# Attention scores and value products of a fused decoder layer in three passes of high and low operands

## What is computed

```python
qkv = jnp.einsum('bsh,ph->bsp', x, weight_qkv).reshape(b, s, NKV, GROUP)   # NKV = 4 groups
q = qkv[..., :QPG * D].reshape(b, s, NKV, QPG, D)                          # 4 query heads each, D = 128
k = qkv[..., QPG * D:(QPG + 1) * D]
v = qkv[..., (QPG + 1) * D:]
scores = jnp.einsum('bsgqd,btgd->bgqst', q, k) * scale
scores = jnp.where(causal, scores, jnp.finfo(scores.dtype).min)
attn = jax.nn.softmax(scores, axis=-1)
out = jnp.einsum('bgqst,btgd->bsgqd', attn, v)
return jnp.einsum('bse,he->bsh', out.reshape(b, s, NH * D), weight_proj)
```

## Time and profile before

| | us |
|---|---|
| median of 3 runs | 1920.68 |
| lowest and highest | 1916.56, 1920.68 |
| profiled execution, its own time | 1925.99 |
| its span, first to last instruction | 1924.0 |
| PE busy | 1846.8 (96%) |
| DVE busy | 1064.5 (55%) |
| ACT busy | 966.6 (50%) |

### The profile page before, as it was taken

The page is one execution under the profiler, slowest core; times in us unless marked ns, Lnnn a source line. Parts: engine busy times, 40 slices in busy tenths (PEclk is TensorE's granted clock), DMA queues, the critical chain, the costliest instruction groups (busy, mean ns, idle before and its releaser), DMA issues. The chain is left out here.

```text
span 1924.0 us, 28232 instructions
## 1 busy us (share of the span) xinstructions
PE 1846.8 (96%) x9769; PEld 1307.8 (68%) x9769; DVE 1064.5 (55%) x2125; ACT 966.6 (50%) x1789; POOL 283.2 (15%) x783
## 2 busy tenths in 40 slices
PE   6999999998999999998998989989989999999998
PEld 4677777776777777764544434434469999999998
DVE  7433443443433434454676867767853336776766
ACT  3533434443434444343576766767753126666651
POOL 1000000000000000042144343343210600000015
PEclk9999999999999999998999999999989999999999
DMA  3100000000100000000000033000010437887756
GB/s 142 34 1 1 23 1 34 1 1 24 34 1 1 22 1 1 1 12 1 1 1 6 2 126 140 0 0 1 1 47 1 183 112 255 291 287 276 273 171 226
DMA packets 73383, 131.54 MB, mean 68 GB/s; under 512 B 4512, under 2 KB 35232, under 8 KB 73248
## 3 DMA queue, kind: packets, MB, share of 16 engines
q1 hardware_dynamic: 68128, 113.01, 17.0%
q0 software_dynamic: 5120, 16.78, 2.6%
HBM read 96.75 MB, written 33.03 MB: 67 GB/s over the span
## 5 line engine op out<-in xcount | busy, mean ns | idle before, releaser
L1561 DVE TENSOR_REDUCE xmax<-ps 128x1 f32<-128x512 f32 x512 | 330.9, 682 | 120.2 <-PE ps L1121 111.0
L1387 ACT ACTIVATE xp<-ps 128x1024 f32<-128x1024 f32 x256 | 263.4, 1031 | 105.9 <-PE ps L1132 104.2
L1319 ACT ACTIVATE probs<-ps,nmax 128x128 f32<-128x128 f32 (+3 forms) x256 | 135.3, 528 | 298.6 <-DVE nmax L1534 297.7
L1534 DVE TENSOR_REDUCE nmax<-ps 128x1 f32<-128x128 f32 (+3 forms) x256 | 124.9, 488 | 238.5 <-PE ps L963 237.4
L1121 PE MATMUL ps<-k,q 64*128 64x512 f32 x496 | 217.5, 479 | 5.3 <-DVE xmax L1561 4.8
L1121 PEld LDWEIGHTS ps<-k,q 64*128 64x128 f32 x496 | 86.8, 188 | 170.6 <-DVE xmax L1561 134.8
L963 PE MATMUL ps<-k_t,q_t 128*128 128x128 f32 (+3 forms) x512 | 198.3, 470 | 0.0
L1132 PE MATMUL ps<-q3m,k 64*128 64x512 f32 x512 | 183.4, 455 | 0.0
L1041 PE MATMUL ps<-pt,v_s 128*128 128x128 f32 (+3 forms) x512 | 159.8, 457 | 2.2 <-ACT pt L1357 1.9
L158 PE MATMUL ps<-ident,probs 128*128 128x128 f32 x704 | 125.1, 282 | 27.3 <-DVE probs L1499 14.8
L158 PEld LDWEIGHTS ps<-ident,probs 128*128 128x128 f32 x704 | 89.6, 144 | 79.8 <-issue 46.8
(11 more groups left out here) (179 smaller groups left out, 3343.5 us busy)
## 6 DMA issues: line engine op xcount, KB each, us to landing
w_raw<-in_w_t SPq DMA_DIRECT2D x56, 704.0 KB, 6.0
w_raw<-in_w_t SPq DMA_DIRECT2D x28, 768.0 KB, 5.9
rows_x<-w_raw SPq DMA_DIRECT2D x1, 9984.0 KB, 29.9
mixed<-rows_x SPq DMA_DIRECT2D x39, 256.0 KB, 4.5
rows_y<-y_s SPq DMA_DIRECT2D x39, 256.0 KB, 5.4
w_raw<-in_w_qkv_t SPq DMA_DIRECT2D x4, 1536.0 KB, 6.8
res<-in_x SPq DMA_DIRECT2D x4, 1024.0 KB, 12.4
w_raw<-in_w_proj_t SPq DMA_DIRECT2D x4, 1024.0 KB, 5.5
```

Of the source, the lines that this page charges most:

```text
L1319: act.activation(probs[:, u % 4, 0:w], ps[:, S_BANK + u % 2, 0:w], ACT.Exp, bias=nmax[:, u % 4:u % 4 + 1], accum_out=rsum[:, u % 4:u % 4 + ...
L1387: act.activation(xp[:, kv % 2, 2 * pair:2 * pair + 2, t, :], ps[:, XST + 2 * (t % 2):XST + 2 * (t % 2) + 2, :], ACT.Exp, scale=X_SCALE).th ...
L1534: dve.tensor_reduce(nmax[:, u % 4:u % 4 + 1], ps[:, S_BANK + u % 2, 0:w], AX_X, ALU.max, negate=True).then_inc(s_max, 1)
L1561: dve.tensor_reduce(xmax[:, slot, i, h:h + 1], ps[:, bank + u % 2, :], AX_X, ALU.max, negate=True).then_inc(s_xmax, 1)
```

## The change

Every operand of the scores and of the products with the values is now kept as two float32r tensors, a high half that ACT rounds from PSUM and a low half that DVE subtracts (PSUM less the high half): `kh`/`kl`, `qh`/`ql`, `vh`/`vl`, `pth`/`ptl`. Each float32 product becomes three float32r products: high·high, high·low, low·high. PE waits for the low half (`s_ql` for a projection, `s_tl` for a turned tile or turned values), where it waited for ACT's copy (`s_q`, `s_te`). The queries have one buffer in place of two, and the turned shares lie tile after tile. The raw weights lie where `wl` and `wol` are written ("in place"), each with a place of its own; six DMAs, one a projection, take the place of one, and SP waits with each until the old low half was last used.

```diff
+            def low_chain(piece, b, bank, value):
+                dve.wait_ge(s_q, value)
+                src = ps[:, G_BANK + bank, :]
+                if piece == 0:
+                    ins = dve.tensor_tensor(kl[:, b % 2, :], src, kh[:, b % 2, :].bitcast(F32), ALU.subtract)
+                else:
+                    h = PROJ_ORDER[piece]
+                    ins = dve.scalar_tensor_tensor(ql[:, h, :], src, ATT_SCALE, qh[:, h, :].bitcast(F32), ALU.mult,
+                                                   ALU.subtract)
+                ins.then_inc(s_ql, 1)
+
+            def low_values(b, bank, value):
+                dve.wait_ge(s_te, value)
+                dve.tensor_tensor(vl[:, b % 2, :, :], ps[:, T_BANK + bank, :].rearrange("p (j d) -> p j d", j=TOK_TILES),
+                                  vh[:, b % 2, :, :].bitcast(F32), ALU.subtract).then_inc(s_tl, 1)
...
             for n in range(NPROJ):
                 split_in(n, n + 1)
+            low_chain(0, 0, 0, 1)
             moments_of(1)
...
-                pe.matmul(ps[:, S_BANK + u % 2, 0:w], q_t[:, b % 2, h, i * P:w], k_t[:, b % 2, 0:w],
-                          start=False, stop=True, skip_group_check=True).then_inc(s_s, 1)
+                for q, kk in ((qh, kh), (qh, kl), (ql, kh)):
+                    ins = pe.matmul(ps[:, S_BANK + u % 2, 0:w], q[:, h, i * P:w], kk[:, b % 2, 0:w],
+                                    start=False, stop=True, skip_group_check=True)
+                ins.then_inc(s_s, 1)
...
                     elif op[0] == "turn":
                         pe.wait_ge(s_pn, N_UNIT * g + op[1] + 1)
-                        pe.wait_ge(s_te, turns_done(g, t) - 1)
+                        pe.wait_ge(s_tl, turns_done(g, t) - 1)
...
-                        pe.wait_ge(s_te, turns_done(g, t))
+                        pe.wait_ge(s_tl, turns_done(g, t))
 
                         for j in reversed(range(TOK_TILES)):
-                            ins = pe.matmul(ps[:, O_BANK + h % 2, j * P:], v_s[:, b % 2, j, :], pt[:, j, j * P:],
-                                            start=(j == TOK_TILES - 1), stop=True, skip_group_check=True)
+                            for v, p in ((vh, pth), (vl, pth), (vh, ptl)):
+                                ins = pe.matmul(ps[:, O_BANK + h % 2, j * P:], v[:, b % 2, j, :],
+                                                p[:, 4 * j:3 * j + TOK_TILES, :].rearrange("p i n -> p (i n)"),
...
             def split_in(n, value):
+                act.wait_ge(s_wp[n], value)
                 act.copy(wh[:, :, columns(n)], w_raw[:, :, columns(n)]).then_inc(s_wh, 1)
...
+                    if op[0] == "turn":
+                        i = op[1] % TOK_TILES
+                        dve.wait_ge(s_te, turns_done(g, t) + 1)
+                        dve.tensor_tensor(ptl[:, i:4 * i + 1:3, :],
+                                          ps[:, T_BANK + (1 + t) % 2, 0:(i + 1) * P].rearrange("p (j n) -> p j n", n=P),
+                                          pth[:, i:4 * i + 1:3, :].bitcast(F32), ALU.subtract).then_inc(s_tl, 1)
+                    elif op[0] == "chain" and is_chain(op):
+                        if op[1] != "v":
+                            low_chain(piece_of(op[1]), op[2], c % 2, N_QKV * g + NPROJ + k + 1)
+                    elif op[0] == "chain":
+                        low_values(op[2], (1 + t) % 2, turns_done(g, t) + 1)
...
+            for g in range(GROUPS - 1):
+                for n in range(NPROJ):
+                    sp.wait_ge(s_g, chains_done(g, last_use(n)))
+                    sp.dma_start(w_raw[:, :, columns(n)], w_v[g + 1][:, :, columns(n)]).then_inc(s_wp[n], 16)
+
+                sp.wait_ge(s_g, chains_done(g + 1, TOK_TILES - 1))
+                sp.dma_start(wo_raw[:, :, :], wo_v[g + 1]).then_inc(s_wo, 16)
```

More of the change, by code:

```diff
@@ L131, in turns_done, with lows_of, last_use @@
     return N_TURN * g + t + 1
+def lows_of(g, k):
+    return (NPROJ - 1) * (1 + BATCH * g + k // NPROJ) + k % NPROJ - (k % NPROJ > 1)
+def last_use(piece):
+    return [c for op, c, t, k in walk(MIDDLE) if op[0] == "chain" and op[2] == BATCH - 1 and is_chain(op)][piece]
 def piece_of(name):
@@ L427, in build @@
         s_out = sem("s_out")
-        s_w = sem("s_w")
+        s_wp = [sem(f"s_wp{n}") for n in range(NPROJ)]
+        s_wo = sem("s_wo")
         s_wh = sem("s_wh")
@@ L442, in build @@
         s_q = sem("s_q")
+        s_ql = sem("s_ql")
+        s_tl = sem("s_tl")
         s_res = sem("s_res")
@@ L636, in _ @@
                 if b == 0:
[L637 to L644, removed]
+                    for n in range(NPROJ):
+                        sp.dma_start(w_raw[:, :, columns(n)], w_v[0][:, :, columns(n)]).then_inc(s_wp[n], 16)
+            sp.dma_start(wo_raw[:, :, :], wo_v[0]).then_inc(s_wo, 16)
+            for g in range(GROUPS - 1):
+                for n in range(NPROJ):
+                    sp.wait_ge(s_g, chains_done(g, last_use(n)))
+                    sp.dma_start(w_raw[:, :, columns(n)], w_v[g + 1][:, :, columns(n)]).then_inc(s_wp[n], 16)
+                sp.wait_ge(s_g, chains_done(g + 1, TOK_TILES - 1))
+                sp.dma_start(wo_raw[:, :, :], wo_v[g + 1]).then_inc(s_wo, 16)
             sp.wait_ge(s_q, N_QKV * GROUPS)
@@ L1503, in turnable @@
                     dve.wait_ge(s_xt, t - 3)
[L1504 to L1510 removed]
+                normal(staged[:, t % 4, :], t).then_inc(s_xn, 1)
+            def low_chain(piece, b, bank, value):
[12 more added lines that the diff above has]
+                                  vh[:, b % 2, :, :].bitcast(F32), ALU.subtract).then_inc(s_tl, 1)
+            def lows(b):
+                for t in range(b * TOK_TILES, (b + 1) * TOK_TILES):
+                    turnable(t)
+                if b:
+                    low_chain(b + 1 + (b > 1), 0, (b + 1 + (b > 1)) % 2, b + 2 + (b > 1))
+                for t in range(b * TOK_TILES, (b + 1) * TOK_TILES):
+                    low(t)
+                if b == 1:
+                    low_chain(3, 0, 1, 4)
             def split(dst, hi, raw, value):
```

82 lines of the change are left out of this document (45 added, 37 removed).

## The result

| | before | after |
|---|---|---|
| median, us | 1919.85 (4 runs) | 2003.34 (4 runs) |
| lowest, highest | 1916.56, 1920.68 | 2001.29, 2004.72 |
| profiled execution, its own time | 1925.99 | 2001.29 |
| mean granted clock | 0.980 | 0.964 |

The change costs 4.4%: the ratio is 1.0437, with an interval of 1.0419 to 1.0455. The forecast was 1991 us in a range of 1940 to 2034. Direction, mechanism and range held; the time came 12 us higher.

What follows compares the result with a forecast made beforehand. PE was taken to bound the attention, with DVE's low halves making it wait: 49 (waits less savings) + 5 (edges) + 6 (start) + 10 (clock) = +70 us, giving 1991 us; own range 1965 to 2015, eight in ten 1940 to 2034.

Steps and rivals of the forecast that it cites:

- A: Steps 9 and 13: products with the values wait for the query's and tile's low halves, +1.0 us, twice a batch.
- B: Steps 14 to 1, without chains: low halves delay the turn of 512 columns and the products with the values, +2.7 us.
- C: Step 12: the turn of 384 columns waits for the low half of the tile two turns back, +0.8 us.
- D: First output of a batch waits for `al`, which DVE reaches later: a guess of +0.2 us.
- The edges: First batch lacks outputs to cover step 5 (+1), last lacks projection chains and has cross-attention work on DVE (+4): +5 us.
- The clock: Waits at the end of a batch make the clock fall after 4 or 5 of 16 batches, 2 to 3 us each: +10.
- At nothing: Six weight DMAs, output weights, the single query buffer and later stages were taken to cost no time.
- 1 (narrow products slow): Rival: three 128-column products cost 0.68 us against 0.33, 45 us over 64 heads: 2025 to 2035 us; chance 0.14.
- 2 (a fall in nearly every batch): Rival: the clock falls in nearly every attention batch, adding 54 us: 2035 us; chance 0.10.
- 3 (half the waits): Rival: DVE's instructions overlap more or ACT's come sooner, halving the waits, few falls: 1936 to 1945 us; chance 0.12.
- 4 (faster): Rival: low halves ready in time, waits below 2.6 us a batch: 1886, or 1853 by pass count; chance together 0.05.
- 5: Rival: the three products run at float32's rate, so nothing is saved: 1991 + 41 us and more; chance 0.02.

Runs made afterwards that it cites:

- e3: Changed kernel with the eight products with the values that need only the high half issued first, the four reading `ptl` last: 1952.97 us, ratio 1.0154.
- e4: Kernel before with three float32r passes of the same high-half operands, no low halves made: 1894.0 us, ratio 0.9847.
- e2: Changed kernel with low halves made and waited for but not read, scores and products with the values one float32 product each: 2022.77 us, ratio 1.051.
- e7: Changed kernel with DVE making k's low half after the second batch's moments in the start, not before them: ratio 1.0379.
- e1: Changed kernel with the turned tile's low half subtracted on one column only, the third product reading the high half again: 1949.98 us, ratio 1.0128.
- e6: Changed kernel with e5's later projection chains and e3's split of the products with the values: 1948.83 us, ratio 0.9971.
- e9: Changed kernel with e3's split, e7's start, e10's chain plan, and low halves of tiles 0 to 2 made later: ratio 0.9913; run again, 0.992.
- e5: Changed kernel with projection chains q0 to q3 moved to steps 9, 11, 13, 15 and the values' turning to step 10: 1978.16 us, ratio 1.0118.
- e10: Kernel before with only the chain steps moved: k 7, v 8, q0 and the values' turn 10, q1 11, q2 13, q3 15: ratio 0.9952.

## Why the prediction was right, and where its terms were off

**The bound.** Right. PE's pace set the attention, DVE had room in the mean (rows of after: 30 to 33 of 57 us; forecast 32), and the question was where DVE's work stood. e3 shows it directly: the same work of DVE, 51 us less. The added work itself came to 157 us in the attention, 9.8 a batch, for a forecast of 12: each subtraction takes what was forecast (0.28, 0.42, 0.56 and 0.69 us), but in a queue the next one starts some 0.08 before it ends.

**What PE saves.** The price of a product alone was right: 128-column float32r products start 0.11 apart. The price of a set was not, for the scores. PE's timeline in after, a score of 512 and one of 256 columns with what follows:

```profile
317.01 0.48 PE L993 MATMUL ps<-kh,qh 128*128 128x512 f32 x1
317.33 0.40 PE L993 MATMUL ps<-kl,qh 128*128 128x512 f32 x1
317.56 0.40 PE L993 MATMUL ps<-kh,ql 128*128 128x512 f32 x1
317.80 1.09 PE L163 MATMUL ps<-xh,wh 128*128 128x512 f32 x4
...
322.88 0.36 PE L993 MATMUL ps<-kh,qh 128*128 128x256 f32 x1
323.08 0.28 PE L993 MATMUL ps<-kl,qh 128*128 128x256 f32 x1
323.20 0.28 PE L993 MATMUL ps<-kh,ql 128*128 128x256 f32 x1
323.31 1.09 PE L163 MATMUL ps<-xh,wh 128*128 128x512 f32 x4
```

The second product follows the first by 0.32 and 0.20 us, the third the second by 0.23 and 0.12: the first of each score takes 0.08 or 0.09 more. Its load of 0.19 us starts with the mask, at 316.99, only 0.02 ahead of it, where those of the other two start 0.23 ahead. Sets of 512 and 256 columns take 0.79 and 0.43 where I had 0.68 and 0.36; those of 384 and 128 take 0.60 and 0.37. That is about 0.3 a head over my prices, and I had put in 0.07: scores save 0.19 a head, not 0.33. At 128 columns three passes (0.37) even cost more than one float32 product (0.28).

For the products with the values the price of 1.95 was right, and the float32 time beside it was not. In e4, and in before at the same step (the rows of 323.23 and 325.39 above):

```profile
313.39 2.08 PE L1044 MATMUL ps<-pt,v_s 128*128 128x128 f32 x12
315.31 0.27 PE L158 MATMUL ps<-ident,probs 128*128 128x128 f32 x1
```

Twelve products take 315.31 - 313.39 = 1.92 us, four float32 ones 325.39 - 323.23 = 2.16. The 2.26 of the earlier trace rows belong to a run that started right behind ACT's copy; in after such a run takes 2.02. So they save 0.24 a head, not 0.31.

A head saves 0.43 us by these starts, and 1.7 / 4 = 0.42 by e4's batches, not 0.64: **27 us, not 41**. The range for it, -4 to 56, had held it. The Trainium skill's rule in "FP8 and Floating Point Precision", section "TensorE Precision Notes", that float32 is four passes, agrees with the products by themselves at 256 to 512 columns (0.49 is four times 0.12, 0.91 four times 0.228), and not at 128 (0.28 against 0.11). A saving of a quarter, 74 us, does not follow from it here: e4 has nothing but ACT's copies in its way, and its whole attention is 33 us shorter.

**The waits.** A to C were where they were forecast. A: 0.94 where I had 1.1, twice. B: 1.18 + 1.62 - 0.18 = 2.6, forecast 2.7. C: the turns wait 10.7 us for `ptl`, 0.67 a batch, forecast 0.8. D: outputs wait 2.3 us in the whole attention, as before (2.5); the guess of 0.2 a batch was wrong, though small. The products with the values wait 54.8 us for `ptl` in all, where I had named some 70 as the sign. Together 80 / 16 = **5.0 a batch, forecast 5.7**, and 5.0 again between e4 and an undisturbed batch of after. (In an undisturbed batch itself PE is idle 5.3 us longer than in before and busy 2.0 less, which is the same net.)

So the net of an undisturbed batch, +3.3 for a forecast of +3.1, came out of two errors that cancel: the saving 0.9 too large, the waits 0.7 too large. A forecast whose sum fits is no proof of its terms; only e4 and e2 took them apart.

**The edges.** First batch 47.1 against 42.1 (89.1 - 47.0; the 42.4 beside the list of masks was a slip), last one 60.5 against 56.4. Beyond the 3.3 of every batch that is 2.5, forecast 5, and in it are 10 us more at half clock.

**The clock.** Its term was too small, and a second error hid that. The attention has 16 falls where before had 4, so 12 more, not 4 or 5; 13 of the 16 batches have one. A fall of 3.4 us adds some 1.4 us of busy time and makes a batch 0.9 to 2.0 us longer, not 2 to 3. In the fourteen batches between the first and the last, PE's busy time above that of an undisturbed batch is 20 us in after and 2.7 in before, so the falls cost 17 there and some 4 at the edges: about **+21, forecast +10**. What took from it again is the batch at 463.0 in before. Its 7 us over the others are 2.7 of busy time and 4.6 of idleness, and most of that is two waits for which the profile shows no cause:

```profile
466.06 0.23 PE L962 MATMUL ps<-mask,ident_b 128*128 128x128 bf16 x1 [2.20 <-issue]
...
469.30 1.01 PE L158 MATMUL ps<-ident,probs 128*128 128x128 f32 x4 [2.53 <-issue]
```

In after the same batch, at 508.2, is idle only 1.3 us more than its neighbours: there the waits for DVE and these fall together. So the batches of after lie above 56.6 by 21 us and those of before above 53.3 by 8, a difference of 13 that looks like the forecast by luck. Here is one fall, behind place B of the batch at 626.2 in after:

```profile
626.00:628.00 2.00, 1.58 (x14) 1.34 (x12) 1.19 (x4) 0.86 (x2) 0.00 (x0) 1.00 0.00 0
628.00:630.00 2.00, 1.25 (x8) 0.96 (x8) 1.62 (x7) 0.98 (x4) 0.00 (x0) 1.00 0.00 0
630.00:632.00 2.00, 0.36 (x3) 0.33 (x2) 1.29 (x4) 0.89 (x3) 0.00 (x0) 0.90 0.00 0
632.00:634.00 2.00, 2.00 (x9) 2.00 (x9) 0.50 (x3) 0.67 (x2) 0.00 (x0) 0.50 0.00 0
634.00:636.00 2.00, 2.00 (x9) 1.61 (x9) 0.00 (x0) 0.59 (x2) 0.00 (x0) 0.74 0.00 0
```

PE works less and less over six us, the clock falls to 1.2 GHz at 631.6, and the products that had waited run at that for 3.4 us. Undisturbed batches have the same waits at the same place; why these are spared is open.

**The start.** +9.0, forecast +6. The term of 2.9 for k's low half was the wrong one: e7 gets 5.5 back for it. The delay itself was sized right, but a longer wait of PE (4.42 us at 31.93, against 1.55 in the earlier trace rows) let the clock fall from 30.9 to 37.7 us (and again from 44.5 to 47.9), and the 16 transposes took 3.68 us, not 2.02. The other low halves cost 3.5, forecast 3.3.

**At nothing.** Right. Each of the 24 pieces of the weights lands in 2.8 us, the output weights in 5.3, and PE's groups in the attention show no wait for either. The stages behind the attention became 2 us shorter, which is within what they differ by in other kernels on one chip (1019.9 us in e1, 1027.5 in e2).

**The 12 us.** The sum against the profiled execution gave 1996, and it took 2001.29: the terms are 5 us short, over the start (3) and the attention (68.4 for 64), less 2 of the rest. Within the attention the terms were further off than their sum: the saving 14 short, the waits 11 less, the clock 11 more, the edges without their falls some 7 less, and 3 less for the batch of 508.2. The other 7 us lie in the step from that execution to a median. I took off 5.3, by which the profiled execution of before stood above its median; that of after stands 2 below its own. The offset of one execution did not carry over; with nothing taken off the forecast would have been 1996.

**The rivals.** 1 (narrow products slow) is refuted by the starts 0.11 apart, 2 (a fall in nearly every batch) is half right: 13 of 16 batches had one, which is close to what I had named as a sign of being wrong, but the price was well under the 3.4 assumed. 3 (half the waits) and 4 (faster) fall by the 80 us of idleness. 5 falls by e4 and e2. Yet rival 4's condition, waits below what is saved, is what e6 and e9 bring about by order alone.

## What to carry to other kernels

A low half made by a second engine costs little as work and much as a stop between two steps of the first engine; issue what needs only the high half first, put independent work where the low half is being made, and in the helper engine's queue let nothing without haste stand ahead of what others wait for. Price a set of short products with its first load, and not by the mean of a long run of them. Before giving the gain to a new form of the computation, run the old form in the new order: here more than half of it was the order's.

## What the runs showed of the hardware that I had not expected

- A fall of the clock followed waits of 1.2 and 1.6 us with work between them, and made a batch 0.9 to 2.0 us longer. Sixteen of them came to 78.5 us at half clock, against 23.9. With shorter waits and the chains moved it was 20.5 (e6).
- Three float32r products of 128 columns took 0.37 us behind the mask, one float32 product 0.28; at 512 columns it was 0.79 against 0.91.
- From e5 to e6 PE's busy time fell by 21 us, with 47.5 us less at half clock, and the waits by 7.5.
- Moving the projection chains in the otherwise unchanged kernel (e10) shortened its attention by 14.6 us, with as much idle time of PE as before. About half of that is the clock. The rest is 0.65 us of busy time in every batch, in part short waits for ACT's copies that the records hide.
